# Another order of the first DMAs, of ScalarE's early copies and of TensorE's early picks in a fused embedding and interaction kernel

## What is computed

```python
e = stack([tbl_m[ids[:, m]] for m in range(32)], axis=1)      # (1024, 32, 16)
x0 = xk = e
for W in (W0, W1, W2):                                        # (32, 32 or 64, 64)
    xk = relu(einsum('bmd,bhd,mhk->bkd', x0, xk, W))
    outs.append(sum(xk, axis=2))
h = concatenate([concatenate(outs, axis=1), dense_ctx], axis=1)   # (1024, 208)
h = maximum(h @ W_top1 + b_top1, 0); h = maximum(h @ W_top2 + b_top2, 0)
y = h @ W_top3
```

## Time and profile before

| what | value |
|---|---|
| median of 3 runs | 629.13 us |
| the profiled execution | 629.63 us, of which the span of instructions is 627.7 us |
| TensorE (PE) | 585.6 us busy, 93% of the span |
| VectorE (DVE) | 577.4 us busy, 92% |
| GpSimd (POOL) | 497.3 us busy, 79% |
| ScalarE (ACT) | 349.6 us busy, 56% |
| DMA | 95.36 MB moved, mean 152 GB/s |
| mean granted TensorE clock | 0.984 |

### The profile page before, as it was taken

One profiled execution on the slowest core, in us unless ns is written; L12 is line 12 of the kernel. 1 busy time (PEld: TensorE's weight loads), 2 busy tenths in 40 slices (PEclk: granted clock), 3 DMA queues, 4 the chain that ended last, 5 costly groups with the idle time before them and its releaser, 6 DMA issues. The chain is left out here.

```text
span 627.7 us, 8728 instructions
## 1 busy us (share of the span) xinstructions
PE 585.6 (93%) x3126; PEld 214.1 (34%) x3126; DVE 577.4 (92%) x582; ACT 349.6 (56%) x535; POOL 497.3 (79%) x349
## 2 busy tenths in 40 slices
PE   3485689999999899999999999999999999999998
PEld 3361223222442224322342224322442234333444
DVE  5567599899999999999999999999999999999993
ACT  0105174745755667635755666635755666756741
POOL 6753579799888988899888988898888896668770
PEclk9879979999999999999999999999999999999999
DMA  4689979940499928993599727980699728990000
GB/s 110 129 165 236 251 119 272 294 118 4 77 237 224 191 19 185 231 240 58 81 243 247 159 28 198 296 210 3 114 236 242 138 28 202 237 247 3 1 2 1
DMA packets 89326, 95.36 MB, mean 152 GB/s; under 512 B 59597, under 2 KB 68338, under 8 KB 89282
## 3 DMA queue, kind: packets, MB, share of 16 engines
q1 hardware_dynamic: 78590, 90.55, 62.8%
q0 software_dynamic: 7104, 1.83, 3.9%
q10 hardware_dynamic: 3588, 2.41, 1.5%
HBM read 91.35 MB, written 3.94 MB: 152 GB/s over the span
## 5 line engine op out<-in xcount | busy, mean ns | idle before, releaser
L1110 DVE TENSOR_TENSOR z<-xk,x0rep 128x1024 f32<-128x1024 f32 x457 | 522.9, 1223 | 19.8 <-issue 9.6
L753 PE MATMUL acc<-z,w_sb 128*64 128x512 f32 x1828 | 433.6, 599 | 20.4 <-DVE z L1110 17.3
L554 POOL TENSOR_TENSOR z_pool<-x0rep,xk_copy 128x1024 f32<-128x1024 f32 x119 | 283.3, 2381 | 55.7 <-PE acc L753 27.9
L504 POOL DMA_INDIRECT emb<-tbl,idx x222 | 213.0, 959 | 58.4 <-issue 48.3
L753 PEld LDWEIGHTS acc<-z,w_sb 128*64 128x64 f32 x1828 | 123.7, 137 | 294.9 <-issue 161.2
L847 ACT ACTIVATE xk<-xk_copy 32x1024 f32<-32x1024 f32 x128 | 130.5, 1019 | 94.3 <-DVE z L1110 93.1
L753 PE MATMUL acc<-z_pool,w_sb 128*64 128x512 f32 x476 | 122.5, 593 | 0.0
L861 ACT ACTIVATE xk_copy<-acc 64x512 f32<-64x512 f32 x128 | 75.2, 588 | 3.7 <-PE acc L753 2.2
L842 ACT ACTIVATE xk<-lay 128x1024 f32<-128x1024 f32 x15 | 15.4, 1027 | 75.7 <-DVE z L1110 75.7
L753 PEld LDWEIGHTS acc<-z_pool,w_sb 128*64 128x64 f32 x476 | 33.7, 137 | 65.1 <-issue 62.8
L823 ACT ACTIVATE xk<-xk_copy 128x1024 f32<-128x1024 f32 x31 | 31.9, 1028 | 14.2 <-DVE z L1110 13.9
(11 more groups left out here) (67 smaller groups left out, 140.6 us busy)
## 6 DMA issues: line engine op xcount, KB each, us to landing
x0rep<-x_rows SPq DMA_DIRECT2D x128, 512.0 KB, 20.7
lay<-x_rows SPq DMA_DIRECT2D x30, 512.0 KB, 6.9
emb<-tbl,idx POOLq DMA_INDIRECT x222, 3.5
squares<-x_rows SPq DMA_DIRECT2D x16, 128.0 KB, 8.6
x_rows<-emb SPq DMA_DIRECT2D x7, 256.0 KB, 4.6
x_rows<-emb SPq DMA_DIRECT2D x9, 128.0 KB, 5.9
w_wrap<-w ACTq DMA_DIRECT2D x4, 128.0 KB, 9.7
w_sb<-w ACTq DMA_DIRECT2D x8, 64.0 KB
```

What stands on the lines that cost most here:

```text
L504: pool.indirect_dma_start(out=emb[:, i % 2, m, :], out_offset=None, in_=tables[m], in_offset=bass.IndirectOffsetOnAxis(ap=idx[:, i, m:m + ...
L554: pool.tensor_mul(z_pool[:, (count - 1) % POOL_RING, :], x0rep[:, g % X0_GROUPS, slot, :], xk_copy[:, side, :]).then_inc(z_pool_ready, 1)
L753: mm = pe.matmul(bank[c * H:(c + 1) * H, :], w[:, tile, :], src[:, c * COLS:(c + 1) * COLS], start=(k == 0), stop=last)
L1110: dve.tensor_mul(z[:, (count - 1) % RING, :], xk[:, bank, :], src).then_inc(z_ready, 1)
```

## The change

- SP's queue: the second group of ids is only tile 1's (new semaphore idx_second_in); the table group 0 goes ahead of w0a and w0b; table group 1 follows the ids of tile 1; then SP waits for w0_summed and stores W0 twice; then table groups 2 to 5, the two stores of W1's wrap, and the ids of tiles 2 to 7 last (idx_in).
- save_first no longer waits for its stores itself. Between the first stores and their wait SP issues two of the W0 loads; two more stand behind the even x0 slots; ScalarE issues twelve instead of ten (eight ahead of copy_rows(0), four behind).
- The two stores of W2's wrap are issued by SP behind the odd x0 slots of side A, not by ScalarE in phase 1.
- ScalarE issues half of W1's STRAIGHT loads ahead of copy_rows(1), half behind it, and the WRAPPED ones behind square(0, A).
- TensorE does pick(3) and pick(4) ahead of spread_lines(6) and turn_rows(0), pick(5) ahead of select_rows(0), pick(6) ahead of spread_lines(8).
- VectorE waits for tile 1's ids and splits them behind pick_rows(2), not ahead of pick_rows(0). GpSimd waits for the later ids at its first gather of tile 2.

```diff
-W0_LOADS = 10
+W0_LOADS = 12
...
+        def make_wrap(queue, wrap, src, done):
+
+            for at, t in ((0, TILES - WRAP // 2), (WRAP // 2, 0)):
+                queue.dma_start(bass.AP(wrap, at * H, [[WRAP * H, P], [1, WRAP // 2 * H]]),
+                                src[:, t:t + WRAP // 2, :].rearrange("p t k -> p (t k)")).then_inc(done, 16)
...
             sp.dma_start(idx[:, 0, :], ids[0:P, :]).then_inc(idx_first_in, 16)
+            load_lines(sp, False, 0)
             for dst, src in ((w0a_sb, w0a), (w0b_sb, w0b)):
                 sp.dma_start(dst, src).then_inc(w0ab_in, 16)
-            load_lines(sp, False, 0)
-            sp.dma_start(idx[:, 1:NT, :], ids[P:B, :].rearrange("(t p) m -> p t m", p=P)).then_inc(idx_in, 16)
-            for g in range(1, len(PICKED)):
-                load_lines(sp, False, g)
+            sp.dma_start(idx[:, 1, :], ids[P:2 * P, :]).then_inc(idx_second_in, 16)
+            load_lines(sp, False, 1)
             sp.wait_ge(w0_summed, 2)
             for n in range(2):
                 sp.dma_start(w0_twice[:, n, :].rearrange("q (r t k) -> q r t k", r=M, t=TILES0), w0a_sb).then_inc(w0_twice_in, 16)
+            for g in range(2, len(PICKED)):
+                load_lines(sp, False, g)
+            make_wrap(sp, w1_wrap, w1, w1_wrap_in)
+            sp.dma_start(idx[:, 2:NT, :], ids[2 * P:B, :].rearrange("(t p) m -> p t m", p=P)).then_inc(idx_in, 16)
...
-                sp.wait_ge(saved_first, 32 * (odd + 1))

             save_first(0)
+            sp.wait_ge(w0_twice_in, 32)
+            load_w0(sp, W0_LOADS, W0_LOADS + 2)
+            sp.wait_ge(saved_first, 32)
             for slot in range(0, SLOTS, 2):
                 load_x0(0, A, slot)
-            load_w0(sp, W0_LOADS, TILES0 * P // M)
+            load_w0(sp, W0_LOADS + 2, TILES0 * P // M)
             save_first(1)
+            sp.wait_ge(saved_first, 64)
             for slot in range(1, SLOTS, 2):
                 load_x0(0, A, slot)
                 if slot == 1:
                     load_rows(0, A)
+            make_wrap(sp, w2_wrap, w2, w2_wrap_in)
             load_side(0, Bs)
...
-            pool.wait_ge(idx_in, 16)
+            pool.wait_ge(idx_second_in, 16)
...
                     if j == 2:
+                        pool.wait_ge(idx_in, 16)
                         pool.wait_ge(saved_first, 16 * FIRST_SAVES)
...
             pick(2)
+            pick(3)
+            pick(4)
             spread_lines(6)
-            pick(3)
             turn_rows(0)
-            pick(4)
+            pick(5)
             spread_lines(7)
             select_rows(0)
-            pick(5)
+            pick(6)
             spread_lines(8)
-            pick(6)
             turn_rows(1)
...
-            load_w0(act, 0, W0_LOADS - 2)
+            load_w0(act, 0, 8)
             copy_rows(0)
-            load_w0(act, W0_LOADS - 2, W0_LOADS)
-            make_wrap(w1_wrap, w1, w1_wrap_in)
-            load_w(w1_sb, w1.tensor, TILES, w1_in, STRAIGHT)
+            load_w0(act, 8, W0_LOADS)
+            load_w(w1_sb, w1.tensor, TILES, w1_in, STRAIGHT[:2])
             copy_rows(1)
-            act.wait_ge(w1_wrap_in, 32)
-            load_w(w1_sb, w1_wrap, WRAP, w1_in, WRAPPED)
+            load_w(w1_sb, w1.tensor, TILES, w1_in, STRAIGHT[2:])
...
             square(0, A)
+            act.wait_ge(w1_wrap_in, 32)
+            load_w(w1_sb, w1_wrap, WRAP, w1_in, WRAPPED)
...
                 if n == 1:
-                    make_wrap(w2_wrap, w2, w2_wrap_in)
...
-            dve.wait_ge(idx_in, 16)
-            split_ids(1)
             for q in range(7):
+                if q == 3:
+                    dve.wait_ge(idx_second_in, 16)
+                    split_ids(1)
                 pick_rows(q)
```

More of the change, by code:

```diff
@@ L298, in build @@
         idx_first_in = sem("idx_first_in")
+        idx_second_in = sem("idx_second_in")
         idx_in = sem("idx_in")
@@ L761, in _ @@
         def _(act):
-            def make_wrap(wrap, src, done):
-                for at, t in ((0, TILES - WRAP // 2), (WRAP // 2, 0)):
-                    act.dma_start(bass.AP(wrap, at * H, [[WRAP * H, P], [1, WRAP // 2 * H]]),
-                                  src[:, t:t + WRAP // 2, :].rearrange("p t k -> p (t k)")).then_inc(done, 16)
             def load_w(dst, src, tiles, done, pieces):
```

## The result

The changed kernel takes **633.25 us** (median of 6 runs, 632.45 to 634.08) beside 629.91 (6 runs) for the kernel before: a ratio of 1.0047, interval 1.0028 to 1.0065. It is slower by a little under 0.5%; I had forecast 620.6. (In this and all later ratios, executions that took over 1.5% longer than the fastest of the same kernel are left out.) Its profiled execution took 633.34 us with a span of 631.5; the same 95.36 MB moved and the busy times of TensorE's matmuls, VectorE, ScalarE and GpSimd are the same within 0.5 us. So the time went in the stages that wait.

A forecast was written before the change was run, and what follows sets the result against it. VectorE is full behind phase 6's step, so only that counts: 110.7 for 119.15, 8.5 us earlier. Span 627.7 - 8.5 = 619.2, plus 1.93 is 621.1, median 0.5 below: 620.6 us, range 615.5 to 627.0.

The forecast's parts named there:

- what bounds the kernel: VectorE is full behind its phase 6 step at 119.15 us, so only idle time left there counts.
- the odd rows' store, 4.3 us: Phase 0: SyncE goes on after this store at 38.6 instead of 42.94; odd slots 4.3 us earlier, bounds 1.5 and 6.
- W1's last loads: Issued behind the square, they land at about 52; cost to TensorE 0 to 5 us, unfelt by VectorE, taken as nothing.
- Phase 2, forecast at 69.6: VectorE idles 1.6 us instead of 6.88, so phase 2 begins 8.6 us earlier, at 69.6 instead of 78.15.
- phase 3, "16.7 us behind the last issue": TensorE's phase 3 start: W2's last issue at 62.2 plus 16.7 us, so 78.9 instead of 87.36.
- VectorE's own way of 33.6 us: VectorE's path to phase 6's step: 33.6 us from 74.5, thus 108.1; TensorE's 110.7 is later and decides.
- the wrap's move: W2's wrap stored by SyncE: 5.2 us go from ScalarE's queue, 1.2 of issue and 3.98 of waiting.
- my three signs of being wrong: Tables later than 31 us, ctx_t held past 68, or W2 landing after 84.
- The third: Rival: ScalarE's queue starves beside SyncE's 4 KB stream, W1 and W2 late; no change 0.13, slower 0.08.
- Its two cases: Starved queue: WRAPPED loads alone late, W2 at 85.5, 627.3 us; STRAIGHT half late too, W2 at 95, 636.6 us.
- The slower case: STRAIGHT half not out when odd slots start: W1 in at 63, phase 3 7.5 us later, 636.6 us; chance 0.08.
- The first rival: Wrap move saves only issue time, ctx_t held longer, W2 lands at 82.9: gain 4.5 us, 624.6 us; chance 0.17.

The follow-up runs named there:

- only_picks: The kernel before with only TensorE's changed order of picks and spreads: 630.65 us, ratio 0.9998.
- two_slots_third: The changed kernel with only even slots 0 and 2 ahead of the odd rows' store, slots 4 and 6 behind it: 631.11 us, ratio 1.0028.
- only_w1_late: The kernel before with only W1's WRAPPED loads moved behind square(0, A): 635.27 us, ratio 1.0083.
- w1_early: The changed kernel with W1's WRAPPED loads put back ahead of square(0, A): 634.62 us, ratio 1.0073.
- only_w2_wrap: The kernel before with only W2's two wrap stores moved from ScalarE to SyncE, behind the odd slots: 633.34 us, ratio 1.0048.
- before_same_chip: The kernel before itself, unchanged, profiled on the chip of the later runs: 630.03 us.
- w2_early: The changed kernel with all W1 and W2 loads ahead of square(0, A), W2's wrap stored by SyncE behind W1's: 669.23 us, ratio 1.0127.
- w2_split: The changed kernel with W1's WRAPPED and W2's STRAIGHT loads ahead of square(0, A), both wraps one behind the other on SyncE: 651.92 us, ratio 0.9869.
- before_w2_split_two: The kernel before with W2's wrap behind W1's, W2's STRAIGHT loads ahead of the square, changed picks, two even slots ahead of the odd store: 648.86 us, ratio 0.9908.

## Why the prediction was wrong, step by step

**Right: what bounds the kernel.** That only what is left at VectorE's step of phase 6 counts held in every kernel (last column). Right too: the picks are done 8.5 us earlier (pick 5 cleared at 26.91, before 35.42; my forecast of 23.5 was 3.4 us too early), the store is reached at 29.85 (forecast 29), and a gap takes TensorE's clock towards the lower of its levels (0.61 behind the 13.41 us).

**Wrong: the odd rows' store, 4.3 us.** I had SyncE go on at 38.6, and it went on at 42.66. Three parts make up these 4.1 us. The even slots moved as fast as I had them (2.1 MB in 10 us), but from 27 to 37 us, since they were issued at 25.73 and not at 23.9. The store's packets then took 5 us, not 3.3. And from the last packet to SyncE's next issue some 0.8 us went, where I had put 0.3 without a row. I had sized the packets by 3104 in 3.5 us, 890 in a us. Between 36 and 41 us of the changed kernel 2977 went in 5 us, 600 in a us:

```profile
q1 hardware_dynamic: 2977, 0.38, 69.7%
q10 hardware_dynamic: 344, 0.31, 21.8%
q0 software_dynamic: 244, 0.06, 14.6%
```

The company was somewhat thicker there (69 packets of ScalarE's queue and 49 of GpSimd's in a us, before 50 and 35), but that alone doesn't explain it: between 39 and 42 us the store went at half the speed of the kernel before, while q1, q10 and q0 together had the engines busy for 65% only. First after, then before, both from 39 to 42:

```profile
q1 hardware_dynamic: 1480, 0.09, 32.1%
q1 hardware_dynamic: 3012, 0.19, 70.1%
```

Why the second half of the store is slow stays open. The mechanism (the store queues behind the even slots) was in the prediction, and only_picks and two_slots_third confirm it. What was left of 4.3 us was 0.3, below my bound of 1.5. With that the term that carried phases 0 and 1 was gone.

**Wrong: W1's last loads, "I take nothing".** This is one of two steps that turned the sign: alone it makes the kernel slower (only_w1_late), but with it undone the changed kernel is still slower (w1_early, 1.0073), by the next one. I had them land at 52 and they were in at 67.03. I took the rate of ScalarE's queue between 44 and 49 us, 21 packets in a us, but those loads had been issued at 41.88, ahead of the stream, and a third of the 106 packets went before 45, when SyncE's queue had moved 17. Here they are issued at 48.70 into the full stream. In the DMA view of the changed kernel from 48.7 to 54 us queue q10 has no row at all, and then it moves 12 packets in a us. My bound of 5 us was less than half of the 13.41 us that TensorE waited, and my cover (six buffers and a fill) hides a late start of TensorE from VectorE's phase 1, but not from its phase 3, which needs phase 1's end: 67.03 + 20.9 = 87.96. only_w1_late shows the price of this step alone: 0.83%. Phase 2, forecast at 69.6, begins near 77.7 (three of the six steps from 74.19 are still phase 1's).

**Wrong: phase 3, "16.7 us behind the last issue".** ctx_t was reached at 72.27, not at 62.2, and W2 was in at 89.79, not at 78.9. Of the 10.1 us at ctx_t 4.2 are the late phase 0 (the first load of W2 at 57.80, not at 53.6). The others are the WRAPPED issue, which holds its sequencer for 8.95 us instead of 2.60 while eight loads stand ahead of it: the wait for the wrap went, and came back as a wait in the issue. Nor is the distance to the landing a constant. From the end of W2's last issue it is 16.7 us in the kernel before, 17.5 in the changed one, 19.7 in only_w2_wrap, 20.6 in two_slots_third and 14 in only_picks. From its first load it is 29.2 us in the kernel before, 32.0 in the changed one, 30.1 in only_w2_wrap, 29.7 in w1_early, 32.2 in two_slots_third, and 27 in only_picks and before_same_chip. In all of them but two_slots_third W2 is in between 87 and 90, wherever its first load stands between 57.8 and 60.8. From 68 us on ScalarE's queue moves 12 to 29 packets in a us, and 40 to 60 only from 82 to 86 on, when SyncE's stream of 4 KB packets thins out. So the stream and the queue's rate beside it set the landing, not the instant at which the last piece is handed in. That last sentence is a reading of the views; no run changes the end of the stream alone. My other sum, VectorE's own way of 33.6 us, was right but for the stall of 1.9 us that stays in it. So the wrap's move (5.2 us in my sum) brings W2 nothing: with it W2 lands some 2 us later. While ScalarE's queue held the wrap's stores it moved 130 packets from 64 to 66 us in the kernel before, 65 in a us; with only the loads in it, 25. The rule of the Trainium skill that I weighed ("DMA: Bandwidth & Descriptors", section "Issuing engines are not separate DMA queues"), that another issuing engine saves only issue time, was nearer than my sum. Even it was too kind: with the later landing and the clock's fall only_w2_wrap loses 0.48%. One of my bounds was also added up wrongly: a first packet at 59 and 21 us make 80, not 81.5. Of my three signs of being wrong two came true: ctx_t past 68, and W2 after 84.

**The rivals.** The third, that ScalarE's queue starves, has the right mechanism: W2 lands at 89.79, in its span of 85.5 to 95. But I let it decide by W2 alone, from 90.5 on. That point was not reached, and the kernel is slower all the same, by W1 and gate A. Its two cases gave 627.3 and 636.6; 633.25 lies between. The slower case got 0.08 because I counted on the queue being emptied before the odd slots; the half of STRAIGHT was, the WRAPPED loads were not. The first rival was right in one point: time saved on the wrap is waited for elsewhere, though in the issue of the WRAPPED loads and not at ctx_t. Its landing at 82.9 was missed too. The two parts alone cost 0.83% (W1 late) and 0.48% (wrap moved), the whole change, which has both, 0.47%. They act on different gates, and only the later counts.

## What to carry to other kernels

Loads that a second queue issued into a full stream arrived late here, whenever their issue was done: put them ahead of the stream, or count their packets, not their issue time. Moving an issue to another queue moves the wait with it, and can make the landing later. Where a phase has two gates (an engine's own way and a weight's landing) an edit is worth only what it does to the later one, and time won at the earlier one can cost TensorE's clock. Size a transfer by a row in which it meets the same company: W1's loads of 32 partitions moved at 21 packets in a us where they met the stream's beginning, and at 12 inside it.

## What the runs showed of the hardware that I had not expected

- A queue's share beside a full stream goes with the shape of its loads: 7 packets of 1 KB in a us with loads of 16 partitions, 12 with 32 and 24 with up to 64, beside 55 to 69 of 4 KB. That these are 2, 4 and 8 engines is taken from the shapes.
- Loads issued into the full stream show no packet at first: none from 48.7 to 54 us after an issue at 48.70, and none from 56.9 to 62 us in the kernel before after issues from 56.88. What happens in these 5 us no view shows.
- Issues can hold their sequencer when much stands ahead of them in their own queue: 9.07 us for two stores behind four slots (4.77 behind two slots), 8.95 us for four loads behind eight (2.68 for four with nothing ahead), 29.3 us for twelve in w2_early. Compute behind them on ScalarE waits as well.
- On three of the chips TensorE's early instructions come late (the longest idle time that ends with "issue" is 9.8 to 21.6 us), and the kernel before takes 652.6 to 656.1 us instead of 630. The trace doesn't show what they wait for.
- The clock's price doesn't follow the length of the gap: the 12 matmuls behind it took 5.39 us after 3.49, 6.03 and 8.06 us of waiting (w2_split, before_w2_split_two, only_w2_wrap), but 4.43 after 4.74 (w1_early) and 4.66 after 8.29 (two_slots_third).
